# Edge walk of a graph attention layer: a register load moved, logit differences made by TensorE, sums kept in PSUM, a loop body four times as long

## The chip, the cores and the metric

The kernel runs on one core of a Trainium2 chip (trn2). The metric is the device time of one execution in microseconds (us); the kernel before has a median of 4355.9 us over three runs (4355.7 to 4357.51).

## What is computed

```python
# graph attention over 200000 edges sorted by dst, 6250 nodes, 8 heads of 32
q, k, v = (xn @ W + b).reshape(n, HEADS, D)            # three products
logits  = einsum('ehd,ehd->eh', q[dst], k[src]) / sqrt(D)
seg_max = segment_max(logits, dst)
expv    = exp(logits - seg_max[dst])
denom   = segment_sum(expv, dst)
agg     = segment_sum(expv / denom[dst] * v[src], dst)
out     = layernorm(x + gelu(agg + skip))
# then a second, smaller attention over 131072 edges routes each node to
# two of four expert networks, whose outputs are added with gates
```

Only the middle of the first half (logits, segment maxima and segment sums) is touched by the change.

## The kernel before, in words

The program has stages in sequence: `prepare` (projections of all nodes to DRAM, walk tables, and the sort of the second edge list), `attend` (the walk over the edges), `node_update`, `route_experts`, `route_gates`. The change lies in `attend` alone, and in the constant PASS (line 43).

**The walk.** Edges are sorted by destination and cut into 391 groups of 512 (G = 4 tiles of 128 edges). Destinations are cut into 49 blocks of 128 nodes. A turn handles one pair of group and node block; where a group spans two blocks it has two turns, so there are 391 + 49 - 1 = 439 turns, and a group has 439/391 = 1.12 turns in the mean. Tables in SBUF (`w_tab`, `g_tab`) give each turn its block and its group; each engine reads them into registers itself (`load`, line 725, a TENSOR_LOAD with an arithmetic operation and a range check behind it).

**What a turn does.** An edge's membership in the block is a one-hot matrix (`oh`, made by ScalarE, turned by TensorE into `ohT`). TensorE spreads the block's queries to edges (12 bf16 products, line 969, into PSUM tile Q). VectorE multiplies them with the gathered keys (`product`, 845) and sums over each head (`logits`, 849). TensorE turns the logits (978), VectorE runs a segmented maximum scan (799), TensorE turns it back (980), VectorE picks the segment ends (792), TensorE collects them per node (998 to 1003), VectorE reduces over the tiles (803) and raises the running maximum of the node block (`raise_max`, 816). TensorE spreads that maximum to the edges (`references`, 986); VectorE subtracts (`difference`, 807, one turn later); ScalarE takes the exponential (922) into the last column of each head of `msg`; VectorE multiplies the gathered values (`message`, 837). TensorE sums messages per node in f32 (1011, 8 instructions), adding the old sums that VectorE has scaled by the fall of the maximum (`scale_sums`, 832, product 1014 with the identity); ScalarE copies the result to the block's place in `acc` in SBUF (899).

**The order.** All of it is a software pipeline written out by hand: in the body for turn s, VectorE works on turns s-1 (message), s (maximum), s+1, s+2 (segment ends, scan) and s+4 (product, logits); TensorE has its own body with turns s-1 to s+7, ScalarE and SyncE likewise. Each engine's body is repeated by `walk` (707): two turns, a loop `Fori` whose body holds PASS = 36 turns, and 5 turns behind it. With 437 turns left after the first two, that is 12 passes. Inside a pass a register once loaded is kept for as many turns as it is needed; `enter` forgets all registers at the head of each pass. The last turn of a pass (`last`) loads nothing for the next.

**The gathers.** GpSimd is not in the loop; its program is unrolled. For each group it issues four indirect DMAs (742) that bring 512 rows of keys and values into a ring of KVR = 8 groups. A slot is free when `message` of its group's last turn is done (740). The group's arrival is passed on to VectorE by the semaphore `tiles` (733), after the four issues of the next group.

**PSUM.** Q takes four banks, `ohT_ps`, `turned_ps`, `node_ps` (references and maxima) and `agg_ps` one each.

Of the kernel before, what the change touches and what calls it, by code (L numbers as in the profile page):

```python
# [26 lines left out]
P = 128  # L27
# [15 lines left out]
PASS = 6 * LOOP  # L43
# [614 lines left out]
def attend(nc, k):  # L658
# [8 lines left out]
    with ExitStack() as ctx:  # L667
# [17 lines left out]
        dl = sb("dl", [P, TG], F32)  # L685
        msg = [sb(f"msg{i}", [P, G, HEADS, HW], F32) for i in range(2)]
        scaled = sb("scaled", [P, HEADS * HW], F32)
# [5 lines left out]
        node_ps = ps("node_ps", [P, 4, P], F32)  # L693
        ref_ps, max_ps = node_ps[:, 0, 0:TG], node_ps[:, 1, 0:TG]
        agg_ps = ps("agg_ps", [P, 512], F32)
        names = ("tiles", "used", "ring_seen", "off", "square", "oh", "turned", "ohT", "q", "prod", "lg", "running", "scans",
                 "seg_max", "maxima", "tile_max", "m_new", "m_fall", "m_all", "fac", "dl", "p", "msg", "oh32", "agg",
                 "scaled", "acc", "cleared", "resets_seen")
# [29 lines left out]
        with nc.Block() as block:  # L728
# [40 lines left out]
            def _(v):  # L769
# [35 lines left out]
                def difference(s):  # L805
                    v.wait_ge(ok["maxima"], s.v + 2)
                    v.tensor_tensor(dl[:, :], lg[s.slot][:, :], ref_ps, ALU.subtract).then_inc(ok["dl"], 1)  # L807

# [3 lines left out]
                def raise_max(s):  # L812
                    v.wait_ge(ok["tile_max"], s.v + 1)
                    if there(s + (-1)):
                        v.wait_ge(ok["m_all"], s.v)
                    v.tensor_tensor(m_new[:, :], node_max(s), tile_max[:, :], ALU.max).then_inc(ok["m_new"], 1)

                def fall(s):
                    v.wait_ge(ok["m_new"], s.v + 1)
                    v.tensor_tensor(m_fall[ring(s, 2)][:, :], node_max(s), m_new[:, :], ALU.subtract).then_inc(ok["m_fall"], 1)  # L820
# [5 lines left out]
                def sums(s):  # L826
                    return k.acc[:, bass.ds(window(s), 1), :].rearrange("p a (h e) -> p (a h) e", e=HW)
# [50 lines left out]
                v.memset(k.acc[:, :, :], 0.0).then_inc(ok["acc"], 1)  # L878
# [962 lines left out]
```

## Time and profile before

| | |
|---|---|
| runs | 4355.9 us median of 3 |
| profiled execution | span 4355.3 us |
| TensorE / VectorE busy in it | 79% / 80% |
| ScalarE / GpSimd busy in it | 58% / 61% |
| stage `prepare` | 0 to 338 us |
| the walk, first to last gather issue | 338.9 to 2667 us |
| the rest (node update, experts, gates) | to 4355 us |

The span holds five stages with different limits, so the shares of the whole say little of the walk; it has to be read in windows of its own. Of a timeline the first column is the start in us from the beginning of the span, the second how long the instruction (or the merged run of instructions) took; the bracket at the end, where there is one, says how long the engine stood idle before it and what ended that. "issue" means that the profile shows nothing that was waited for. Starts of successive VectorE instructions are closer together than the durations, since the next one starts before the last one has written everything; so costs are read from start to start.

### The profile page before, as it was taken

Reading aid. Unit: us, or ns where it says so; the run is one execution under the profiler, and the core shown is the slowest. Engines: PE = TensorE matmul, PEld = TensorE weight load, DVE = VectorE, ACT = ScalarE, POOL = GpSimd, SP = SyncE. Lnnn points to the kernel's source line nnn. Section 1 sums busy time; section 2 is a strip of 40 time slices with the busy share of each in tenths; the row PEclk is TensorE's granted clock in tenths of the full one; section 3 lists DMA queues with packets and bytes.
Section 4 is the critical chain, followed back from the end, with each engine's and each line's share of the span. In section 5 each row is a group of like instructions: output and inputs, shape, how many; then the busy total and the mean of one; then the engine's idle time right before and its main releaser. Section 6 shows DMA issues by size and latency. Waiting matters only on the chain. (4 is left out here: it accounts for less than half of the span.)

```text
span 4355.3 us, 107023 instructions
## 1 busy us (share of the span) xinstructions
PE 3439.8 (79%) x26106; PEld 2517.5 (58%) x26107; DVE 3480.0 (80%) x9712; ACT 2533.3 (58%) x6256; POOL 2677.3 (61%) x2719
## 2 busy tenths in 40 slices
PE   7887988889898988989898888248888888887620
PEld 3335777777777777777777676235555555555410
DVE  8887988889898988989898898866666666666457
ACT  5436766767676766767676676545555555555310
POOL 3226766666666666666666663227777777777740
PEclk9988999999999999999999999559999999999855
DMA  6537777767677767777776774611121111111147
GB/s 222 182 118 231 227 212 220 212 210 227 207 226 215 224 208 214 227 212 218 217 225 207 215 225 152 215 56 26 30 35 31 31 30 31 31 35 30 22 95 274
DMA packets 367763, 677.61 MB, mean 156 GB/s; under 512 B 70294, under 2 KB 240482, under 8 KB 367074
## 3 DMA queue, kind: packets, MB, share of 16 engines
q0 software_dynamic: 157888, 420.64, 35.2%
q1 hardware_dynamic: 183106, 223.48, 15.2%
q10 hardware_dynamic: 26080, 25.70, 2.0%
q8 instruction: 261, 4.28, 0.4%
q14 instruction: 428, 3.51, 0.3%
HBM read 582.00 MB, written 87.58 MB: 154 GB/s over the span
## 5 line engine op out<-in xcount | busy, mean ns | idle before, releaser
L742 POOL DMA_INDIRECT KV<-kv_d,src_i x1564 | 1558.6, 997 | 775.9 <-issue 437.0
L1385 POOL DMA_INDIRECT re_src<-src_tab_d,rsrc x1024 | 985.9, 963 | 312.1 <-issue 245.6
L1011 PE MATMUL agg_ps<-msg,oh 128*128 128x264 f32 x3512 | 865.2, 390 | 2.5 <-DVE msg L837 1.9
L837 DVE TENSOR_TENSOR msg<-KV,msg 128x1024 f32<-128x1024 f32 x439 | 537.9, 1225 | 225.1 <-issue 223.9
L1011 PEld LDWEIGHTS agg_ps<-msg,oh 128*128 128x128 f32 x3512 | 640.4, 192 | 98.8 <-ACT oh L926 2.0
L969 PE MATMUL Q<-q,ohT 128*128 128x256 bf16 x5328 | 672.4, 277 | 1.9 <-issue 0.9
L911 ACT ACTIVATE square<-iota_b,off 128x128 bf16<-128x128 bf16 x1784 | 569.4, 392 | 0.3
L845 DVE TENSOR_TENSOR prod<-KV,Q 128x1024 f32<-128x1024 f32 x443 | 537.8, 1214 | 5.1 <-POOLq L733 3.4
L849 DVE TENSOR_REDUCE lg<-prod 128x32 f32<-128x1024 f32 x443 | 535.0, 1208 | 0.2
L969 PEld LDWEIGHTS Q<-q,ohT 128*128 128x128 bf16 x5328 | 495.7, 99 | 64.2 <-issue 2.2
L922 ACT ACTIVATE msg<-dl 128x32 f32<-128x32 f32 x439 | 113.4, 258 | 662.3 <-DVE dl L807 662.3
L1593 PE MATMUL ex_y_ps<-ex_w,ex_hid 128*112 128x256 f32 x1792 | 441.2, 390 | 0.0
L1581 PE MATMUL ex_h<-acc,ex_w 128*128 (+1 forms) x896 | 413.9, 587 | 4.1 <-PEq L1094 3.5
L1512 ACT COPY re_ohT<-re_ohT_ps 128x1024 bf16<-128x1024 bf16 x179 | 181.2, 1012 | 348.8 <-PE re_ohT_ps L1555 348.0
L1593 PEld LDWEIGHTS ex_y_ps<-ex_w,ex_hid 128*112 128x112 f32 x1792 | 302.7, 179 | 53.8
L914 ACT ACTIVATE oh<-square,one 128x512 bf16<-128x512 bf16 x446 | 322.0, 722 | 14.5
L978 PE MATMUL turned_ps<-ident,lg 128*32 128x128 f32 x442 | 120.4, 272 | 257.2 <-DVE running L799 251.2
L926 ACT CAST oh<-oh 128x512 f32<-128x512 bf16 x439 | 272.0, 620 | 0.0
L1014 PE MATMUL agg_ps<-scaled,ident 128*128 128x264 f32 x878 | 267.1, 386 | 0.0
L1418 DVE TENSOR_SCALAR re_oh<-iota_b,re_off 128x128 bf16<-128x128 bf16 x1432 | 252.6, 274 | 6.4
L918 ACT COPY ohT<-ohT_ps 128x512 bf16<-128x512 bf16 x445 | 251.2, 564 | 4.8 <-PE ohT_ps L959 4.8
L1555 PE MATMUL re_ohT_ps<-ident_b,re_oh 128*128 128x128 bf16 x1432 | 120.4, 232 | 162.0 <-DVE re_oh L1418 157.7
(261 smaller groups left out, 5864.4 us busy)
## 6 DMA issues: line engine op xcount, KB each, us to landing
q<-q_d SPq DMA_DIRECT2D x446, 192.0 KB
y_d<-ex_y ACTq DMA_DIRECT2D x56, 448.0 KB
rg_ye<-y_d SPq DMA_DIRECT2D x7, 3584.0 KB, 12.5
KV<-kv_d,src_i POOLq DMA_INDIRECT x1564
nu_xs<-xs_d SPq DMA_DIRECT2D x7, 2688.0 KB, 11.7
re_src<-src_tab_d,rsrc POOLq DMA_INDIRECT x1024
kv_d<-pr_kv SPq DMA_DIRECT2D x49, 256.0 KB, 2.2
xs_d<-pr_xs SPq DMA_DIRECT2D x49, 256.0 KB, 2.3
```

Of the source, the lines that this page charges most:

```text
L742: pool.indirect_dma_start(out=KV[:, t % (KVR * G), :], out_offset=None, in_=k.kv_d, in_offset=bass.IndirectOffsetOnAxis(ap=k.src_i[:, t:t ...
L837: v.tensor_tensor(m[:, :, :, 0:DH], KV[:, tiles(s), D:2 * D].rearrange("p t (h d) -> p t h d", d=DH), bc(m[:, :, :, DH:HW], [P, G, HEADS, ...
L845: v.tensor_tensor(prod[:, :, :], KV[:, tiles(s), 0:D], Q[ring(s, 2)][:, :, :], ALU.mult).then_inc(ok["prod"], 1)
L849: v.reduce_sum(lg[s.slot][:, :], prod[:, :, :].rearrange("p t (h d) -> p (t h) d", d=DH), AX.X).then_inc(ok["lg"], 1)
L911: q = act.activation(square[:, t, :], k.iota_b[:, :], ACT.Square, bias=off[s.slot][:, t:t + 1])
L914: act.activation(oh[ring(s, OHR)][:, :, :], square[:, :, :], ACT.Relu, bias=k.one[:, :], scale=-1.0).then_inc(ok["oh"], 1)
L926: act.copy(oh32[ring(s, 2)][:, :, :], oh[ring(s, OHR)][:, :, :]).then_inc(ok["oh32"], 1)
L969: m = pe.matmul(Q[ring(s, 2)][:, t, :], ohT[ring(s, OHR)][:, t, :], q3[s.slot][:, c * D:(c + 1) * D], start=(c == 0), stop=(c == 2))
L1011: pe.matmul(agg_ps[:, 0:HEADS * HW], oh32[ring(s, 2)][:, t, :], msg[ring(s, 2)][:, t, :, :].rearrange("p h e -> p (h e)"), start=(t == 0), ...
L1385: pool.indirect_dma_start(out=gs[:, t % (RING * RG), :], out_offset=None, in_=k.src_tab_d, in_offset=bass.IndirectOffsetOnAxis(ap=k.rsrc[: ...
L1581: m = pe.matmul(h_ps[f % 2][:, 0:UN], k.w1_sb[:, u.at % NE, c, f * P:(f + 1) * P], k.xT[:, bass.ds(u.block, 1), c, half * UN:(half + 1) * ...
L1593: m = pe.matmul(y_ps[w % 2][0:YN, 0:D], hid[u.at % 2][:, f, w * YN:(w + 1) * YN], k.w2_sb[:, u.at % NE, f, :], start=(f == 0), stop=(f == ...
```

## The change

Four things are done at once:

1. VectorE's load of the next turn's block number (`window(s + 1)`) goes from behind `raise_max`, ahead of `message`, to behind `product`, ahead of `logits`.
2. VectorE's `difference` is gone. TensorE's `references` is now `differences`: it puts the logits into `dl_ps` through a product with the f32 identity (128x32) and adds the four spread maxima. For that the running maximum is kept with its sign turned (`raise_max` becomes one scalar_tensor_tensor, `fall` and the first value of `m_all` turn too). It waits until ScalarE has read the differences of the turn before. ScalarE's exponential reads `dl_ps` from PSUM.
3. The sums stay in `agg_ps`: `scale_sums` multiplies that tile in place and is placed right behind `message`; the two instructions of line 1014 are gone; `sums` waits for the scaling before its first product. ScalarE still copies the sums to `acc` in each turn, and `scale_sums` waits for the copy of the turn before. `acc` (49 x 264 columns) is no longer cleared; TensorE makes the first zeros in `agg_ps` by one product with 264 cleared columns. A new block's first fall is so large that its factor is 0.
4. PASS is 144 instead of 36: three passes instead of twelve, still 5 turns behind them.

`max_ps` moves into the bank of `turned_ps`; `dl_ps` has the bank that `node_ps` had.

```diff
-PASS = 6 * LOOP
+PASS = 24 * LOOP
...
-                def difference(s):
-                    v.wait_ge(ok["maxima"], s.v + 2)
-                    v.tensor_tensor(dl[:, :], lg[s.slot][:, :], ref_ps, ALU.subtract).then_inc(ok["dl"], 1)
...
-                    v.tensor_tensor(m_new[:, :], node_max(s), tile_max[:, :], ALU.max).then_inc(ok["m_new"], 1)
+                    v.scalar_tensor_tensor(out=m_new[:, :], in0=tile_max[:, :], scalar=-1.0, in1=node_max(s),
+                                           op0=ALU.mult, op1=ALU.min).then_inc(ok["m_new"], 1)
...
                 def scale_sums(s):
                     v.wait_ge(ok["fac"], s.v + 1)
-                    v.wait_ge(ok["acc"], s.v + 1)
-                    v.tensor_tensor(scaled[:, :].rearrange("p (h e) -> p h e", e=HW), sums(s), bc(fac[ring(s, 2)][:, :].unsqueeze(2), [P, HEADS, HW]), ALU.mult).then_inc(ok["scaled"], 1)
+                    if there(s + (-1)):
+                        v.wait_ge(ok["acc"], s.v)
+                    else:
+                        v.wait_ge(ok["emptied"], 1)
+                    sums = agg_ps[:, 0:HEADS * HW].rearrange("p (h e) -> p h e", e=HW)
+                    v.tensor_tensor(sums, sums, bc(fac[ring(s, 2)][:, :].unsqueeze(2), [P, HEADS, HW]), ALU.mult).then_inc(ok["scaled"], 1)
...
                 def body(s, last):
                     if there(s):
                         tile_maxima(s)
-                    if there(s + (-1)):
-                        difference(s + (-1))
                     if there(s + 1):
                         segment_max(s + 1)
                     if there(s + 2):
                         scan(s + 2)
                     if there(s):
                         raise_max(s)
-                    if there(s) and not last:
-                        window(s + 1)
                     if there(s + (-1)):
                         message(s + (-1))
+                        scale_sums(s + (-1))
                     if there(s):
                         fall(s)
                     product(s + 4)
-                    if there(s + (-1)):
-                        scale_sums(s + (-1))
+                    if there(s) and not last:
+                        window(s + 1)
                     logits(s + 4)
...
-                v.memset(k.acc[:, :, :], 0.0).then_inc(ok["acc"], 1)
-                v.memset(k.m_all[:, :, :], -BIG).then_inc(ok["cleared"], 1)
+                v.memset(msg[1][:, 0, :, :], 0.0).then_inc(ok["cleared"], 1)
+                v.memset(k.m_all[:, :, :], 2.0 * BIG).then_inc(ok["cleared"], 1)
...
-                def references(s):
+                def differences(s):
                     pe.wait_ge(ok["m_new"], s.v + 1)
+                    if there(s + (-1)):
+                        pe.wait_ge(ok["p"], s.v)
+                    pe.matmul(dl_ps, k.ident[:, :], lg[s.slot][:, :], start=True, stop=False)
                     for t in range(G):
-                        pe.matmul(ref_ps[:, t * HEADS:(t + 1) * HEADS], ohT[ring(s, OHR)][:, t, :], m_new[:, :], start=True, stop=True)
+                        m = pe.matmul(dl_ps[:, t * HEADS:(t + 1) * HEADS], ohT[ring(s, OHR)][:, t, :], m_new[:, :],
+                                      start=False, stop=(t == G - 1))
+                    m.then_inc(ok["dl"], 1)
...
-                    pe.wait_ge(ok["acc"], s.v + 1)
+                    pe.wait_ge(ok["scaled"], s.v + 1)
                     for t in range(G):
-                        pe.matmul(agg_ps[:, 0:HEADS * HW], oh32[ring(s, 2)][:, t, :],
-                                      msg[ring(s, 2)][:, t, :, :].rearrange("p h e -> p (h e)"), start=(t == 0), stop=False)
-                    pe.wait_ge(ok["scaled"], s.v + 1)
-                    pe.matmul(agg_ps[:, 0:HEADS * HW], k.ident[:, :], scaled[:, :], start=False, stop=True).then_inc(ok["agg"], 1)
+                        m = pe.matmul(agg_ps[:, 0:HEADS * HW], oh32[ring(s, 2)][:, t, :],
+                                      msg[ring(s, 2)][:, t, :, :].rearrange("p h e -> p (h e)"), start=False, stop=(t == G - 1), skip_group_check=True)
+                    m.then_inc(ok["agg"], 1)
```

## Rows read from the trace of the kernel before

**Rows 1.** Windows view, one pass: busy us (instructions) PE, PEld, DVE, ACT, POOL; clock, DMA, GB/s.
```profile
555.40:747.60 192.20, 170.30 (x1478) 137.98 (x1476) 169.21 (x397) 133.14 (x396) 127.32 (x128) 0.98 0.72 217
```
**Rows 2.** Timeline of VectorE, one ordinary turn and the head of the next.
```profile
2005.84 0.18 DVE L803 TENSOR_REDUCE tile_max<-node_ps 128x8 f32<-128x32 f32 x1
2005.94 0.18 DVE L807 TENSOR_TENSOR dl<-lg,node_ps 128x32 f32<-128x32 f32 x1
...
2006.13 0.40 DVE L799 TENSOR_TENSOR_SCAN running<-reset,turned_ps 32x128 f32<-32x128 f32 x1
2006.46 0.13 DVE L816 TENSOR_TENSOR m_new<-m_all,tile_max 128x8 bf16<-128x8 f32 x1
2007.03 1.23 DVE L837 TENSOR_TENSOR msg<-KV,msg 128x1024 f32<-128x1024 f32 x1 [0.44 <-issue]
2008.17 0.16 DVE L820 TENSOR_TENSOR m_fall<-m_all,m_new 128x8 f32<-128x8 bf16 x1
2008.25 1.22 DVE L845 TENSOR_TENSOR prod<-KV,Q 128x1024 f32<-128x1024 f32 x1
2009.38 0.43 DVE L832 TENSOR_TENSOR scaled<-acc,fac 128x264 f32<-128x264 f32 x1
2009.72 1.21 DVE L849 TENSOR_REDUCE lg<-prod 128x32 f32<-128x1024 f32 x1
2010.92 0.31 DVE L803 TENSOR_REDUCE tile_max<-node_ps 128x8 f32<-128x32 f32 x1
```
**Rows 3.** Timeline of VectorE, the last turn of the last pass (loads nothing).
```profile
2675.48 0.18 DVE L803 TENSOR_REDUCE tile_max<-node_ps 128x8 f32<-128x32 f32 x1
...
2676.10 0.13 DVE L816 TENSOR_TENSOR m_new<-m_all,tile_max 128x8 bf16<-128x8 f32 x1
2676.20 1.23 DVE L837 TENSOR_TENSOR msg<-KV,msg 128x1024 f32<-128x1024 f32 x1
...
2680.09 0.18 DVE L803 TENSOR_REDUCE tile_max<-node_ps 128x8 f32<-128x32 f32 x1
```
**Rows 4.** Timeline of VectorE: the jump between two passes, and the next pass's end.
```profile
752.76 0.31 DVE L803 TENSOR_REDUCE tile_max<-node_ps 128x8 f32<-128x32 f32 x1
...
760.81 0.19 DVE L803 TENSOR_REDUCE tile_max<-node_ps 128x8 f32<-128x32 f32 x1 [3.23 <-issue]
...
790.36 0.18 DVE L803 TENSOR_REDUCE tile_max<-node_ps 128x8 f32<-128x32 f32 x1
...
944.87 0.31 DVE L803 TENSOR_REDUCE tile_max<-node_ps 128x8 f32<-128x32 f32 x1
```
**Rows 5.** Timeline of TensorE, the same ordinary turn.
```profile
2006.68 0.27 PE L978 MATMUL turned_ps<-ident,lg 128*32 128x128 f32 x1 [0.43 <-DVE running L799]
...
2008.74 1.95 PE L1011 MATMUL agg_ps<-msg,oh 128*128 128x264 f32 x8
2010.52 0.61 PE L1014 MATMUL agg_ps<-scaled,ident 128*128 128x264 f32 x2
2010.97 0.39 PE L959 MATMUL ohT_ps<-ident_b,oh 128*128 128x128 bf16 x4
2011.76 0.27 PE L978 MATMUL turned_ps<-ident,lg 128*32 128x128 f32 x1 [0.41 <-DVE running L799]
```
**Rows 6.** Timeline of ScalarE, the same ordinary turn.
```profile
2006.29 0.36 ACT L899 COPY acc<-agg_ps 128x264 f32 x1
```
**Rows 7.** Timeline of GpSimd, first issues of two successive groups in the start.
```profile
349.28 0.94 POOL L742 DMA_INDIRECT KV<-kv_d,src_i  x1 [0.30 <-issue]
...
354.29 0.95 POOL L742 DMA_INDIRECT KV<-kv_d,src_i  x1 [0.30 <-issue]
```
**Rows 8.** Waits of GpSimd, 560 to 2640 us: us in total, times, longest us.
```profile
POOL KV L742 <- DVE msg L837: 276.5, 65, 6.7
```
**Rows 9.** Timeline of VectorE, the start of the walk.
```profile
340.87 10.84 DVE L878 MEMSET acc<- 128x12936 f32 x1 [3.05 <-issue]
...
364.19 1.22 DVE L845 TENSOR_TENSOR prod<-KV,Q 128x1024 f32<-128x1024 f32 x1 [2.10 <-POOLq L733]
```

More of the change, by code:

```diff
@@ L684, in attend @@
         fac = [sb(f"fac{i}", [P, HEADS], F32) for i in range(2)]
-        dl = sb("dl", [P, TG], F32)
         msg = [sb(f"msg{i}", [P, G, HEADS, HW], F32) for i in range(2)]
-        scaled = sb("scaled", [P, HEADS * HW], F32)
         KV = sb("KV", [P, KVR * G, 2 * D], F32)
@@ L692, in attend @@
         lgT_ps, runT_ps = turned_ps[0:TG, 0, :], turned_ps[:, 1, 0:TG]
-        node_ps = ps("node_ps", [P, 4, P], F32)
-        ref_ps, max_ps = node_ps[:, 0, 0:TG], node_ps[:, 1, 0:TG]
+        max_ps = turned_ps[:, 2, 0:TG]
+        dl_ps = ps("dl_ps", [P, 512], F32)[:, 0:TG]
         agg_ps = ps("agg_ps", [P, 512], F32)
-        names = ("tiles", "used", "ring_seen", "off", "square", "oh", "turned", "ohT", "q", "prod", "lg", "running", "scans",
+        names = ("tiles", "used", "off", "square", "oh", "turned", "ohT", "q", "prod", "lg", "running", "scans",
                  "seg_max", "maxima", "tile_max", "m_new", "m_fall", "m_all", "fac", "dl", "p", "msg", "oh32", "agg",
-                 "scaled", "acc", "cleared", "resets_seen")
+                 "scaled", "acc", "cleared", "emptied", "resets_seen")
         ok = {n: nc.alloc_semaphore(f"at_{n}") for n in names}
@@ L815, in raise_max @@
                         v.wait_ge(ok["m_all"], s.v)
-                    v.tensor_tensor(m_new[:, :], node_max(s), tile_max[:, :], ALU.max).then_inc(ok["m_new"], 1)
+                    v.scalar_tensor_tensor(out=m_new[:, :], in0=tile_max[:, :], scalar=-1.0, in1=node_max(s),
+                                           op0=ALU.mult, op1=ALU.min).then_inc(ok["m_new"], 1)
                 def fall(s):
                     v.wait_ge(ok["m_new"], s.v + 1)
-                    v.tensor_tensor(m_fall[ring(s, 2)][:, :], node_max(s), m_new[:, :], ALU.subtract).then_inc(ok["m_fall"], 1)
+                    v.tensor_tensor(m_fall[ring(s, 2)][:, :], m_new[:, :], node_max(s), ALU.subtract).then_inc(ok["m_fall"], 1)
                 def keep_max(s):
@@ L824, in keep_max @@
                     v.tensor_scalar(node_max(s), m_new[:, :], 1.0, None, ALU.mult).then_inc(ok["m_all"], 1)
-                def sums(s):
-                    return k.acc[:, bass.ds(window(s), 1), :].rearrange("p a (h e) -> p (a h) e", e=HW)
                 def scale_sums(s):
                     v.wait_ge(ok["fac"], s.v + 1)
-                    v.wait_ge(ok["acc"], s.v + 1)
-                    v.tensor_tensor(scaled[:, :].rearrange("p (h e) -> p h e", e=HW), sums(s), bc(fac[ring(s, 2)][:, :].unsqueeze(2), [P, HEADS, HW]), ALU.mult).then_inc(ok["scaled"], 1)
+                    if there(s + (-1)):
[4 more added lines that the diff above has]
+                    v.tensor_tensor(sums, sums, bc(fac[ring(s, 2)][:, :].unsqueeze(2), [P, HEADS, HW]), ALU.mult).then_inc(ok["scaled"], 1)
                 def message(s):
@@ L876, in body @@
                         group(s + 5)
-                v.memset(k.acc[:, :, :], 0.0).then_inc(ok["acc"], 1)
-                v.memset(k.m_all[:, :, :], -BIG).then_inc(ok["cleared"], 1)
-                v.wait_ge(ok["cleared"], 1)
+                v.memset(msg[1][:, 0, :, :], 0.0).then_inc(ok["cleared"], 1)
+                v.memset(k.m_all[:, :, :], 2.0 * BIG).then_inc(ok["cleared"], 1)
+                v.wait_ge(ok["cleared"], 2)
                 walk(v, body, 4, enter)
                 enter()
-                difference(LAST)
                 message(LAST)
@@ L921, in weights @@
                     act.wait_ge(ok["dl"], s.v + 1)
-                    act.activation(msg[ring(s, 2)][:, :, :, DH:HW], dl[:, :].rearrange("p (t h a) -> p t h a", h=HEADS, a=1), ACT.Exp,
+                    act.activation(msg[ring(s, 2)][:, :, :, DH:HW], dl_ps.rearrange("p (t h a) -> p t h a", h=HEADS, a=1), ACT.Exp,
                                    scale=SCALE).then_inc(ok["p"], 1)
@@ L1019, in body @@
                     if there(s):
-                        references(s)
+                        differences(s)
                     if there(s + 1):
@@ L1029, in body @@
                         group(s + 2)
+                pe.wait_ge(ok["cleared"], 1)
+                pe.matmul(agg_ps[:, 0:HEADS * HW], k.ident[:, :], msg[1][:, 0, :, :].rearrange("p h e -> p (h e)"),
+                          start=True, stop=True).then_inc(ok["emptied"], 1)
                 walk(pe, body, 7, groups.clear)
```

## Prediction, on record before the changed kernel ran

> **What bounds the kernel now.** I read the page first, then windows by stage, then timelines of one turn on each engine. The page's shares of 79% TensorE and 80% VectorE do not tell which of the two sets the pace, since they are averages over five stages. The window of one pass of 36 turns does better: 192.2 us, a TensorE clock of 0.98 of full speed (so its upper level, 2.4 GHz, nearly throughout), DMA engines 72% busy [rows 1]. From the head of a turn to the head of the next VectorE works without a hole except one: 5.08 us from L803 to L803, in which only `message` (L837) has idle time before it, 0.44 us [rows 2]. TensorE waits once in the turn, for VectorE's scan, 0.41 to 0.43 us [rows 5]. So VectorE sets the pace of the walk; TensorE follows with little to spare. The reader should see that the hole of 0.44 us is called "issue": no semaphore is late, the engine's own sequencer is still busy with the register load that stands ahead of `message` in the program.
>
> The mean ordinary turn is a little over 5.08: thirty turns from 790.36 to 944.87 take 154.51 us, 5.15 each [rows 4].
>
> **Part 1, the load behind `product`.** The kernel before has turns in which this load is missing: the last turn of a pass loads nothing. There L837 starts 0.10 us after L816 instead of 0.57, and the turn takes 4.61 us from L803 to L803 instead of 5.08 [rows 2, 3]. That is the gain to expect, 0.47 us a turn, if the load is hidden in its new place. Its cover there is `product`, 1.13 us from start to start (2008.25 to 2009.38) [rows 2]; the load cost 0.47 of visible time where nothing but the end of a short instruction covered it, so it fits into 1.13 even if it is somewhat longer than what was visible. The instruction behind it, `logits`, has to wait for the end of `product` anyway. If the cover failed (the sequencer reaching the load only when `product` ends) the 0.47 would come back ahead of `logits`.
>
> **Part 2, differences by TensorE.** `difference` occupied VectorE from 2005.94 for about 0.10 us until its successor (L792 starts at the same pitch as L807 behind L803, 0.10) [rows 2]. It goes: 0.10 us a turn. The sign turns cost nothing: one instruction for one, on the same 8 columns.
>
> TensorE gets one f32 product of 32 columns through the identity, as two instructions. No row shows such a one. Bounds: the two instructions of L1014, with the same 128x128 f32 weights but 264 columns, take 0.45 together (2010.52 to 2010.97); at the other end if only the columns counted, 32 of 264 would make it 0.45/8, that is 0.05 [rows 5]. I take 0.25, nearer to the wide weights than to the few columns. The Trainium skill ("TensorE: Matmul & The Clock Gate", section "LDWEIGHTS (loading the stationary operand)") makes a load of 128 columns 128/1.2 = 107 ns, so an estimate by that page is 0.21 us for the two; the sum does not use it.
>
> ScalarE now gets its differences a turn's length earlier than it can use them, from PSUM as it already reads `agg_ps`. At nothing.
>
> **Part 3, sums in PSUM.** TensorE loses the two instructions of L1014, 0.45 us a turn [rows 5]. VectorE's scaling has the same 264 columns; it reads and writes PSUM now. For reading there is a pair of rows: `product` has one operand in PSUM and its successor starts 1.13 us later, `message` has all in SBUF and its successor starts 1.14 us later [rows 2]. So reading costs nothing. No row has VectorE write to PSUM; as upper bound I take the whole pitch of a tiny instruction again, 0.08 us (L820 to L845) [rows 2], lower bound 0; I take 0, since the operand rows show no difference. The Trainium skill says otherwise for operands ("VectorE: DVE Perf Modes", section "The TRN2 errata — SBUF-src ops pay a fixed extra latency per instruction"): a fixed part of 120 cycles from PSUM against 58 from SBUF at 0.96 GHz. That would be 0.065 us a turn, an estimate of 28 us over the walk by this page, and the sum would come out at 4080. The pair of rows above shows nothing of such a difference, so I go by the rows.
>
> The scaling moves ahead of TensorE's eight products, so there is a new chain from turn to turn: scaling, eight products (1.78 from first start to the next instruction, and their latency) [rows 5], ScalarE's copy 0.36 [rows 6], scaling again 0.43 [rows 2]. That is about 3 us, under a turn. In phase it also holds: `message` ends 0.1 us before L820's successor; the products of the turn before have ended by the time TensorE comes to its wait for the scan, the copy follows in half a microsecond, and the scaling comes only 1.2 us after the scan. What queues behind the scaling on VectorE, should it wait, is everything: `fall`, `product`, `logits`.
>
> TensorE's turn: its path without the wait is 5.08 less 0.41 less what the overlap of the last product allows (about 0.15), 4.5 us. Less 0.45, plus 0.25: 4.3, at the upper bound 4.5. VectorE's turn will be 5.15 - 0.47 - 0.10 = 4.58. So VectorE stays the bound, with 0.1 to 0.3 us to spare.
>
> The clearing of `acc` (10.84 us) goes at the start of the walk [rows 9]. It is worth nothing or little: the fourth product, at 364.19, waits 2.10 us for gathers, which GpSimd issues at its own speed from 338.9 on. I count 0; if gathers were not late, at most 10.8.
>
> **Part 4, three passes for twelve.** The jump back costs: six turns from 752.76 to 790.36 take 37.60 us where six ordinary ones of 5.12 (the commonest length in the timeline) take 30.72, so 6.9 us [rows 4]; of that 3.23 is a standstill at the jump, the rest is spread over the next five turns, in which registers are loaded anew and instructions arrive late. The window of the pass says the same: 192.2 us less 36 x 5.15 leaves 6.8 [rows 1]. There are eleven such jumps; counted in this manner over the timeline they cost 6.7 to 7.7, mean 7.04. Two will be left. Nine fewer: 9 x 7.04 = 63.3 us. The entry into the loop and the way out of it stay. I take the cost of a jump as independent of the body's length, since the standstill follows the jump and not the instructions before it.
>
> **The sum.** 438 intervals x 0.57 = 249.7; jumps 63.3; together 313. From this I take off 9 for the gathers, as follows. GpSimd issues a group in 5.01 us (349.28 to 354.29) [rows 7]. With 391 groups to 439 turns that is 4.46 us a turn against 4.58: not the bound, but near. Before, GpSimd stood 276.5 us of 2080 waiting for `message` [rows 8]; that reserve shrinks to some 2%. In a stretch of eight turns without a shared group VectorE wants eight groups in 36.6 us and GpSimd needs 40.1, so it falls behind by 3.5, and catches up in the ninth turn. The ring gives three turns of lead, 13.7 us, from the end of `message` of one group to `product` of the group eight later. In the start, where VectorE waits for them, a group's gathers take 9.9 us from their first issue to its product (354.29 to 364.19) [rows 7, 9]. That leaves 3.8 against the 3.5 by which it falls behind: enough, with now and then a hitch. Nine microseconds, 0.2 for each of 49 node blocks, is my estimate for the hitches and for the start.
>
> The profiled execution has a span of 4355.3 us, and the median of the runs is 4355.9, so both differ by 0.6 and the saving can be taken from the median: 4355.9 - 313 + 9 = 4052 us.
>
> **Rivals.**
>
> *Gathers set the pace* (15%). For it: the reserve of 2% above, and DMA engines that are already 72% busy [rows 1] and have to move the same bytes in 0.89 of the time, near 80%, so that landings may come later. Against: the mean is still under VectorE's. Its time: a turn of 4.68 instead of 4.58, 44 us more, so about 4096, and 4110 if landings take 2 us longer.
>
> *TensorE or the PSUM write set the pace* (14%). For it: both bounds above together, TensorE at 4.5 and each handover late by 0.1 to 0.2; or 0.08 more for the write. Its time: 0.08 to 0.12 a turn, 35 to 53 us, so 4087 to 4105. Against: TensorE loses more than it gets.
>
> *The change doesn't do what it says: the load shows again in front of `logits`* (4%). Then 0.47 x 438 = 206 us come back: 4258. Against: the turns without load, and 1.13 us of cover.
>
> *Slower than before* (3%): the chain through `agg_ps`. VectorE's whole stream stands behind the scaling, the scaling behind ScalarE's copy, the copy behind TensorE's last product of the turn before. If ScalarE came to the copy late, behind its one-hot work, each turn would grow. The point from which it decides: the jumps saved are worth 63.3/438 = 0.14 a turn, so from a turn of 5.15 + 0.14 = 5.29 on the kernel is slower. At a turn of 5.4 it would take 4355.9 + 0.11 x 438 = 4404. Against: the chain adds up to 3 us, and ScalarE's order (weights, copy, then the rest) keeps the copy early.
>
> *Better than forecast* (6%): the small irregularities over 5.08 go too, 0.05 a turn, 4030 or a little less.
>
> **How the numbers follow.** The forecast, 4040 to 4070, has 58%. The range takes in the gathers' and TensorE's cases and the lucky one: 4028 to 4112, leaving out about 4% below and 13% above. A difference under 0.2% (8.7 us) could not be told from none by this measurement; none of the cases but the chain's edge lies there. Faster 0.96, same 0.01, slower 0.03.
>
> **What would show it.** In the changed profile: `message` 0.1 to 0.2 us behind `raise_max`, without idle time before it (part 1); no VectorE instruction between L803 and the segment ends, and the new f32 product within 0.05 to 0.45 on TensorE (part 2); the scaling at a pitch of 0.34 as before (part 3); three standstills of 3 to 4 us on VectorE at most instead of eleven, each with its 7 us (part 4); GpSimd's wait for `message` shrunk from 276 to under 100 us, VectorE rarely waiting for `KV`. Wrong would be: idle time before `product` that ends with gathers in most turns, idle time before the scaling that ends with ScalarE's copy, or idle time before `logits`.

## The result, and the profile after

The changed kernel takes 4241.1 us (median of four runs, 4232.8 to 4248.9), against 4356.7 us of the kernel before in the same comparison: a ratio of 0.9731, interval 0.9716 to 0.9746. In a second comparison on a chip of the same speed it took 4232.7 us, 0.9714 (0.9698 to 0.9731). It is faster by 116 to 123 us, where 304 were forecast; 4241 lies above the whole range. All times below are of executions in the chip's faster state; one, of the changed kernel with passes of 36 turns, took 5439.7 us at a granted TensorE clock of 0.55 against 0.91 to 0.92 in its like, and is left out.

All of it is in the walk. Between the first `tile_max` of the walk and the last (367.19 and 2580.33) lie 2213.1 us, 122.6 less than before (2335.7), or 5.05 us for each of 438 intervals where 4.64 were forecast (jumps and the 9 us for gathers included). The stages behind the walk, which the change doesn't touch, took 1653.0 us before and 1654.6 after (1653.3 in a second profile of the changed kernel); over the versions told below on chips of this speed they vary from 1641 to 1655. So differences of some ten us between versions are read from the walk, not from the whole time.

VectorE's timeline of an ordinary turn of the changed kernel (columns as in [rows 2]):

```profile
1500.24 0.18 DVE L801 TENSOR_REDUCE tile_max<-turned_ps 128x8 f32<-128x32 f32 x1
1500.34 0.18 DVE L790 SCALAR_TENSOR_TENSOR seg_max<-last_b,turned_ps 128x32 bf16<-128x32 f32 x1
1500.44 0.40 DVE L797 TENSOR_TENSOR_SCAN running<-reset,turned_ps 32x128 f32<-32x128 f32 x1
1500.77 0.13 DVE L810 SCALAR_TENSOR_TENSOR m_new<-tile_max,m_all 128x8 bf16<-128x8 f32 x1
1500.82 1.21 DVE L833 TENSOR_TENSOR msg<-KV,msg 128x1024 f32<-128x1024 f32 x1
1501.96 0.42 DVE L828 TENSOR_TENSOR agg_ps<-agg_ps,fac 128x264 f32<-128x264 f32 x1
1502.30 0.14 DVE L815 TENSOR_TENSOR m_fall<-m_new,m_all 128x8 f32<-128x8 bf16 x1
1502.38 1.20 DVE L841 TENSOR_TENSOR prod<-KV,Q 128x1024 f32<-128x1024 f32 x1
1503.61 1.22 DVE L845 TENSOR_REDUCE lg<-prod 128x32 f32<-128x1024 f32 x1
...
1504.82 0.18 DVE L801 TENSOR_REDUCE tile_max<-turned_ps 128x8 f32<-128x32 f32 x1
...
1505.40 1.20 DVE L833 TENSOR_TENSOR msg<-KV,msg 128x1024 f32<-128x1024 f32 x1
...
1517.45 1.22 DVE L841 TENSOR_TENSOR prod<-KV,Q 128x1024 f32<-128x1024 f32 x1 [0.86 <-POOLq L731]
```

This turn takes 4.58 us from L801 to L801, to the hundredth what was forecast (in part by luck, see below). `message` starts 0.05 behind `raise_max` with no idle time (0.57 in [rows 2]). But in the fourth turn from here `product` has stood 0.86 us for L731, the semaphore that says that the group's rows are there. Of the 438 turns 207 are such ordinary ones of 4.58 or 4.59 us; the others are longer, up to 7 us outside the jumps, most often with a wait for rows in them.

The waits of the changed kernel from 560 to 2500 us (us in total, times, longest us), those of VectorE:

```profile
DVE prod L841 <- POOLq L731: 82.4, 95, 2.4
DVE prod L841 <- PE Q L961: 32.5, 29, 2.1
...
DVE agg_ps L828 <- ACT acc L891: 19.1, 26, 2.3
...
DVE tile_max L801 <- issue: 6.8, 2, 3.5
```

GpSimd's wait for `message`, 276.5 us in [rows 8], does not occur in this stretch at all. So the roles have changed: before, GpSimd waited for VectorE; now it never does, and VectorE waits for it.

GpSimd's timeline in the same stretch shows why it doesn't keep up:

```profile
1499.83 0.95 POOL L740 DMA_INDIRECT KV<-kv_d,src_i  x1 [0.30 <-DMA KV<-kv_d,src_i]
1501.08 1.77 POOL L740 DMA_INDIRECT KV<-kv_d,src_i  x1 [0.30 <-issue]
1503.16 0.95 POOL L740 DMA_INDIRECT KV<-kv_d,src_i  x1 [0.31 <-issue]
1504.41 0.95 POOL L740 DMA_INDIRECT KV<-kv_d,src_i  x1 [0.30 <-issue]
1505.67 1.77 POOL L740 DMA_INDIRECT KV<-kv_d,src_i  x1 [0.30 <-issue]
1507.74 0.95 POOL L740 DMA_INDIRECT KV<-kv_d,src_i  x1 [0.31 <-issue]
1508.99 0.94 POOL L740 DMA_INDIRECT KV<-kv_d,src_i  x1 [0.30 <-issue]
1510.24 1.77 POOL L740 DMA_INDIRECT KV<-kv_d,src_i  x1 [0.30 <-issue]
```

Every third issue takes 1.77 us instead of 0.95. It is the one that starts 0.26 us after `message` (1501.08 against 1500.82, 1505.67 against 1505.40). Three issues, one of them long, fill exactly one turn: 1505.67 - 1501.08 = 4.59. So the pattern keeps itself in step as long as VectorE runs undisturbed, and GpSimd then needs 4/3 of 4.58, 6.11 us, for a group. VectorE uses up the lead and waits for rows (1511.92, for 0.32 us, and 1517.45, for 0.86); by that the phase slips, and issues run free for a while.

The kernel before has the same long issue, seldom. Its GpSimd timeline at such a place:

```profile
1949.13 0.95 POOL L742 DMA_INDIRECT KV<-kv_d,src_i  x1 [0.30 <-issue]
1950.38 1.98 POOL L742 DMA_INDIRECT KV<-kv_d,src_i  x1 [0.31 <-issue]
```

and its VectorE timeline at the same place:

```profile
1950.32 1.23 DVE L837 TENSOR_TENSOR msg<-KV,msg 128x1024 f32<-128x1024 f32 x1 [0.45 <-issue]
```

Over all issues behind the first `message`, sorted by how long after the start of the last `message` each begins (worked out from the two timelines; mean duration in us, number in brackets):

| start after `message`, us | before | changed | message reads weights from PSUM |
|---|---|---|---|
| 0.0 to 0.2 | 1.92 (11) | 1.79 (26) | 0.945 (60) |
| 0.2 to 0.4 | 1.69 (13) | 1.76 (242) | 0.945 (54) |
| 0.4 to 0.6 | 1.55 (27) | 1.52 (42) | 0.945 (80) |
| 0.6 to 0.8 | 1.39 (14) | 1.32 (19) | 0.945 (39) |
| 0.8 to 1.0 | 1.07 (231) | 1.13 (35) | 0.946 (50) |
| later | 0.95 to 1.02, and seven of 1.10 to 1.22 | 0.95 to 0.96 | 0.945 |

The last column is an experiment, told below. In the first two, start and duration add up to the same: an issue that begins 0.06 to 1.08 us after `message` began ends 2.03 us after that start (2.05 in the kernel before, whose `message` is 0.02 longer), and so 0.82 after `message` itself (1.21 long) has ended. An issue that begins outside this stretch isn't lengthened, not even just ahead of it: 46 issues of the changed kernel that begin in the last 0.13 us before a `message` take 0.942 to 0.952, and three that begin 0.01 after its start take 0.942 to 0.947 (they are in the first row's mean). That fits an issue that comes, about 0.13 us after its own start (0.95 less 0.82), to something that `message` holds until its end. What that is no row shows. From when on it is held differs: ahead of the second half of a `message` in two parts (an experiment below) issues that begin up to 0.06 us before it are long too. `message` itself does not get longer: 1.207 us in the mean beside an issue of over 1.2 us, 1.214 without one.

The seven late ones in the kernel before obey the same law with another instruction. They begin 0.03 to 0.15 us after `scale_sums`, which there reads both its operands, `acc` and `fac`, from SBUF, and each ends 0.82 us after it has ended. GpSimd's and VectorE's line of one of them:

```profile
1947.66 1.16 POOL L742 DMA_INDIRECT KV<-kv_d,src_i  x1 [0.39 <-issue]
```
```profile
1947.58 0.42 DVE L832 TENSOR_TENSOR scaled<-acc,fac 128x264 f32<-128x264 f32 x1
```

In the changed kernel, whose `scale_sums` reads the sums from PSUM, no issue that begins over 1.1 us after `message` takes more than 0.97.

The groups of instructions (line, count, busy us and mean ns | idle before, by what), GpSimd's gathers in the changed kernel:

```profile
L740 POOL DMA_INDIRECT KV<-kv_d,src_i x1564 | 1738.2, 1111 | 483.4 <-issue 444.4 <-DMA KV<-kv_d,src_i 34.1 <-POOLq L197 4.8
```

and in the kernel before:

```profile
L742 POOL DMA_INDIRECT KV<-kv_d,src_i x1564 | 1558.6, 997 | 775.9 <-issue 437.0 <-DVE msg L837 291.7 <-DMA KV<-kv_d,src_i 42.4
```

1738.2 + 483.4 us are 2221.6, and that is the walk: the gathers are issued without any wait for VectorE from first to last. A turn's share is 2221.6/439 = 5.06, measured 5.05. Undisturbed it would be 1564 x (0.946 + 0.309) = 1963 us, 4.47 a turn, under VectorE's 4.58: that was the forecast's picture.

### The profile page after: what moved, and what is told of

It reads as the page before. It is cut to its first block and busy times, and to the rows that moved or that the text cites. A ratio compares the mean times of both kernels' runs of the same rounds, so it can differ in the third digit from the quotient of the medians.

```text
span 4234.9 us, 106026 instructions
## 1 busy us (share of the span) xinstructions
PE 3355.8 (79%) x26108; PEld 2461.8 (58%) x26109; DVE 3429.0 (81%) x9273; ACT 2556.3 (60%) x6256; POOL 2860.5 (68%) x2719
## 3 DMA queue, kind: packets, MB, share of 16 engines
q1 hardware_dynamic: 183106, 223.48, 15.4%
## 5 line engine op out<-in xcount | busy, mean ns | idle before, releaser
L740 POOL DMA_INDIRECT KV<-kv_d,src_i x1564 | 1738.2, 1111 | 483.4 <-issue 444.4
L1008 PE MATMUL agg_ps<-msg,oh 128*128 128x264 f32 x3512 | 882.1, 395 | 1.6 <-DVE agg_ps L828 1.6
L1008 PEld LDWEIGHTS agg_ps<-msg,oh 128*128 128x128 f32 x3512 | 656.1, 197 | 102.2 <-ACT oh L918 1.7
L961 PE MATMUL Q<-q,ohT 128*128 128x256 bf16 x5328 | 691.4, 282 | 0.5 <-issue 0.3
L891 ACT COPY acc<-agg_ps 128x264 f32 x439 | 166.5, 379 | 474.4 <-PE agg_ps L1008 473.3
L1417 DVE TENSOR_SCALAR re_oh<-iota_b,re_off 128x128 bf16<-128x128 bf16 x1432 | 258.2, 278 | 11.5 <-issue 4.3
L1554 PEld LDWEIGHTS re_ohT_ps<-ident_b,re_oh 128*128 128x128 bf16 x1432 | 87.9, 103 | 247.4 <-DVE re_oh L1417 213.7
```

The lines of the kernel that those rows point to most:

```text
L740: pool.indirect_dma_start(out=KV[:, t % (KVR * G), :], out_offset=None, in_=k.kv_d, in_offset=bass.IndirectOffsetOnAxis(ap=k.src_i[:, t:t ...
L961: m = pe.matmul(Q[ring(s, 2)][:, t, :], ohT[ring(s, OHR)][:, t, :], q3[s.slot][:, c * D:(c + 1) * D], start=(c == 0), stop=(c == 2))
L1008: m = pe.matmul(agg_ps[:, 0:HEADS * HW], oh32[ring(s, 2)][:, t, :], msg[ring(s, 2)][:, t, :, :].rearrange("p h e -> p (h e)"), start=False ...
```

## The experiments

Theory A: `message` with two operands in SBUF stands in the way of the gathers' issues, by the phase law above, and the issues set the pace. Its rivals: B, the DMA engines, which now move 229 GB/s instead of 217 [rows 1], make landings late; C, it is PSUM or TensorE's side of the new chain.

Seven of the runs (told below as "on the slower chips") were made on two chips on which every kernel takes over 5800 us (the kernel before 5954 on the one, 5917 on the other), so that VectorE is late and GpSimd waits for it by far the longest; their times don't bear on the question, and only the durations of their issues are used.

### Message reads its weights from PSUM

ScalarE takes the exponential a second time, into the spare half of the bank of `ohT_ps`, and `message` multiplies with that. It adds waits: TensorE's turn of a one-hot waits for the exponential, `message` for that turn, ScalarE's `turn_copy` for `message`.

```diff
+        w_ps = ohT_bank[:, G, 0:2 * TG].bitcast(F32)
...
                 def message(s):
                     v.wait_ge(ok["p"], s.v + 1)
+                    v.wait_ge(ok["turned"], s.v + 8)
...
-                                    bc(m[:, :, :, DH:HW], [P, G, HEADS, DH]), ALU.mult).then_inc(ok["msg"], 1)
+                                    bc(w_ps.rearrange("p (t h a) -> p t h a", h=HEADS, a=1), [P, G, HEADS, DH]), ALU.mult).then_inc(ok["msg"], 1)
...
                 def weights(s):
+                    act.activation(w_ps, dl_ps, ACT.Exp, scale=SCALE)
```

> The changed kernel, but message reads the edge weights from PSUM (ScalarE writes them there by a second exponential), so it has one operand in SBUF instead of two. Theory A (a gather's issue on GpSimd stands still while message runs, because message reads two operands from SBUF; in the changed kernel 3 gathers instead of 4 get through per turn of 4.58 us): the gathers of 1.77 us disappear, mean issue 0.95 to 0.98 us instead of 1.11, mean turn 4.58 to 4.68 instead of 5.05, time 4050 to 4095 us. Rival B (the DMA queues: 420 MB of rows can't land faster): issue times and time stay as in the changed kernel, 4225 to 4245. Rival C (GpSimd's own pace of four issues is the bound, blocked or not): little gain, 4200 to 4240.

On a slower chip: 5856.5 us against 5954.3, ratio 0.983 (0.978 to 0.988). The mean issue is 946 ns; of 1564 only the first of all is long, as in every kernel (1.30).

> As e1, weights of message from PSUM. Theory A: 4050 to 4095 us where the kernel before takes 4356, gathers 0.95 us each, mean turn 4.58 to 4.68 us. Rivals B (DMA volume) and C (four issues of 1.25 us are too slow anyway): no faster than the changed kernel by more than 40 us.

Measured: 4103.8 us, ratio 0.9418 (0.9402 to 0.9434); 129 to 137 us less than the changed kernel, 9 above what A expected. Its group of gathers:

```profile
L742 POOL DMA_INDIRECT KV<-kv_d,src_i x1564 | 1478.9, 946 | 609.4 <-issue 445.5 <-DVE msg L836 128.0 <-DMA KV<-kv_d,src_i 31.1
```

and its window of 560 to 2400 us (columns as in [rows 1]):

```profile
560.00:2400.00 1840.00, 1717.37 (x15861) 1404.93 (x15859) 1786.87 (x3866) 1479.93 (x4641) 1299.60 (x1375) 1.00 0.80 243
```

GpSimd again waits for `message`, 128 us, and the DMA engines are busier than in the changed kernel, whose window of 560 to 2500 us is:

```profile
560.00:2500.00 1940.00, 1751.83 (x15773) 1428.06 (x15772) 1771.18 (x3847) 1442.49 (x4229) 1521.19 (x1368) 0.97 0.77 229
```

243 GB/s against 229, and VectorE never waits for rows in that window: B is out. A turn is still longer than 4.58 (most take 4.58 to 4.75, the mean with jumps is 4.77). That fits the waits that the edit adds: `message` starts 0.12 to 0.15 us behind `raise_max` around 1505 us, where the changed kernel has 0.05.

### Message in two halves

`message` is two instructions of 512 columns, `scale_sums` between them. Each half holds issues for half as long.

```diff
+                    for a in (0, 2):
+                        w = v.tensor_tensor(m[:, a:a + 2, :, 0:DH], KV[...][:, a:a + 2], bc(m[:, a:a + 2, :, DH:HW], [P, 2, HEADS, DH]), ALU.mult)
+                        if a == 0:
+                            scale_sums(s)
+                    w.then_inc(ok["msg"], 1)
...
                         message(s + (-1))
-                        scale_sums(s + (-1))
```

> The changed kernel, message in two instructions of 512 columns with the scaling of the sums (one operand in PSUM) between them. Theory A: the longest standstill of a gather is halved, longest usual issue 1.3 to 1.5 us instead of 1.77, mean 1.00 to 1.05, mean turn 4.7 to 4.85, time 4090 to 4150. Rival B: no gain, and 0.06 us a turn more on VectorE that is hidden: 4225 to 4245.

On a slower chip: 5832.9 us (two runs), ratio 0.978 (0.972 to 0.984), mean issue 990 ns, a little under the 1.00 to 1.05 expected.

> As e3, message in two halves with the scaling between. Theory A: usual delayed issue 1.24 us (as in e3) instead of 1.77, mean gather 1.00 to 1.03, 4070 to 4150 us where the kernel before takes 4356. Rival B: as the changed kernel.

Measured: 4098.1 us, ratio 0.9408 (0.9392 to 0.9424), faster than both kernels. Its walk is as long as that with weights from PSUM (2087.8 and 2088.3 us from the first `tile_max` to the last); the 6 us between the two are behind the walk. The group of gathers:

```profile
L740 POOL DMA_INDIRECT KV<-kv_d,src_i x1564 | 1592.1, 1018 | 501.6 <-issue 438.9 <-DMA KV<-kv_d,src_i 32.0 <-DVE msg L834 25.8
```

And VectorE's timeline, around one of the few waits for rows:

```profile
1501.58 0.67 DVE L834 TENSOR_TENSOR msg<-KV,msg 128x512 f32<-128x512 f32 x1
1502.18 0.42 DVE L828 TENSOR_TENSOR agg_ps<-agg_ps,fac 128x264 f32<-128x264 f32 x1
1502.52 0.67 DVE L834 TENSOR_TENSOR msg<-KV,msg 128x512 f32<-128x512 f32 x1
1503.12 0.15 DVE L815 TENSOR_TENSOR m_fall<-m_new,m_all 128x8 f32<-128x8 bf16 x1
1503.87 1.22 DVE L845 TENSOR_TENSOR prod<-KV,Q 128x1024 f32<-128x1024 f32 x1 [0.60 <-POOLq L731]
```

The half costs 0.60 from start to start, so a turn has 0.06 more of VectorE. The issues and their gaps, the 25.8 us of waiting for `message` left out, come to (1.018 + 0.304) x 4 = 5.29 a group, 4.71 a turn; the mean turn is 4.77 (2087.8/438). Even here the issues and VectorE (4.64 to 4.70 in most turns) are nearly level.

### Half the bytes

Each gather brings the keys only, 1 KB for each row instead of 2; `message` multiplies the keys. The values are left out; number and length of all instructions stay.

```diff
-                        pool.indirect_dma_start(out=KV[:, t % (KVR * G), :], out_offset=None, in_=k.kv_d,
+                        pool.indirect_dma_start(out=KV[:, t % (KVR * G), 0:D], out_offset=None, in_=k.kv_d,
```

> The changed kernel with gathers of 1 KB rows instead of 2 KB (message multiplies the keys' half again instead of the values): as many issues, half the bytes. Theory A: the same time as the changed kernel within 20 us and the same 1.11 us a gather. Rival B: 100 us or more faster.

Measured: 4245.9 us (two runs), ratio 0.9746 (0.9727 to 0.9766), like the changed kernel, and the issues as long, though the DMA engines now move 136 GB/s instead of 229 in the window of 560 to 2500 us:

```profile
L740 POOL DMA_INDIRECT KV<-kv_d,src_i x1564 | 1752.7, 1121 | 482.0 <-issue 466.5 <-DMA KV<-kv_d,src_i 10.7 <-POOLq L197 4.8
```

What a gather brings plays no part. B is refuted from the other side too.

### The changed kernel again

> The changed kernel itself, so that the runs beside it have their like on the same chip. On a chip like that of the first measurement 4225 to 4250 us against 4356 before, all gathers issued without waiting for message, 1.11 us a gather. On a chip like that of the runs e1 to e4 (before 5954 us) some 5850 to 5900.

4232.7 us, mean issue 1111 ns: the result stands.

### The changed kernel with passes of 36 turns

```diff
-PASS = 24 * LOOP
+PASS = 6 * LOOP
```

> As e9, for a chip on which the kernel before takes 4356 us: the changed kernel with PASS = 36. Theory A: 0 to 25 us over the changed kernel's 4233 to 4241, so 4235 to 4265. Rival (each jump 7 us in any case): about 4298.

Measured: 4243.2 us, ratio 0.974 (0.972 to 0.976), 2 to 11 us more. The walk itself takes 2232.7 us against 2213.1 and 2215.0 in the two profiles of the changed kernel: nine more jumps cost 18 to 20 us there, 2.0 to 2.2 each, and not 63. They are still there on VectorE (turns of 8.2, 7.0, 5.9 and 5.4 us at one), but GpSimd's program is unrolled and goes on issuing meanwhile, and VectorE waits less for rows, as this kernel's waits from 560 to 2500 us show (82.4 us in the changed kernel):

```profile
DVE prod L841 <- POOLq L731: 68.1, 68, 2.7
```

### Weights from PSUM, passes of 36 turns

> As e10: weights of message from PSUM and PASS = 36. VectorE bounds this walk, so the nine jumps cost 50 to 65 us over 4104: 4154 to 4169.

Measured: 4211.0 us, ratio 0.9668 (0.9652 to 0.9684), 107 us more, of which 103.9 are in the walk (2192.2 us against 2088.3): where gathers are not in the way, nine jumps cost 11.5 us each, 104 together where 50 to 65 were expected. Most of the excess is the edit's added wait, which is long at a jump:

```profile
562.93 1.22 DVE L836 TENSOR_TENSOR msg<-KV,ohT_ps 128x1024 f32<-128x1024 f32 x1 [3.90 <-PE ohT_ps L959]
```

The waits of `message` for TensorE, from 400 to 2560 us, grow by it from 15.4 us with two jumps to 59.0 with eleven, 4.8 for each. Without them a jump costs 6.7, near the prediction's 7.04. The expectation's size was wrong; that the jumps are dear here and cheap in the changed kernel held.

### Single parts in the kernel before

Only the pass of 144 turns:

> As e11: the kernel before with PASS = 144 alone. Theory A: 45 to 63 us gained, 4293 to 4311. If gathers were the bound already: under 20 us.

Measured: 4282.0 us, ratio 0.9826 (0.981 to 0.9843): 75 us less, 11 below the lower end of what was expected. The walk is shorter by 64.9 us (2270.9 against 2335.7), 7.2 for each of nine jumps, and part 4 said 63.3 and 7.04; the rest lies behind the walk, where this kernel took 1641.7 us and the kernel before 1653.0. GpSimd's wait for `message` stays the long one, from 560 to 2500 us (261.2 in the same window of the kernel before):

```profile
POOL KV L742 <- DVE msg L837: 194.9, 45, 5.4
```

Only the load moved:

```diff
-                    if there(s) and not last:
-                        window(s + 1)
                     if there(s + (-1)):
                         message(s + (-1))
                     if there(s):
                         fall(s)
                     product(s + 4)
+                    if there(s) and not last:
+                        window(s + 1)
```

> As e12: the kernel before with the load behind product alone. If VectorE's own turn (4.61 to 4.68 us) counted, 4150. Theory A: three issues into such a turn, 4235 to 4290, issues of 1.77 us, mean 1.09 to 1.12.

Measured: 4284.6 us, ratio 0.983 (0.9813 to 0.9846), within what theory A expected: 73 us less, where 438 x 0.47 = 206 of VectorE's time are removed. Without any other part of the change the issues already grow, to a mean of 1145 ns, more than the 1.09 to 1.12 us expected:

```profile
L742 POOL DMA_INDIRECT KV<-kv_d,src_i x1564 | 1790.6, 1145 | 488.0 <-issue 456.1 <-DMA KV<-kv_d,src_i 26.5 <-POOLq L197 4.8
```

and GpSimd's wait for `message` is gone, VectorE's for rows is there (waits from 560 to 2500 us):

```profile
POOL KV L742 <- DVE msg L837: 0.6, 2, 0.3
...
DVE prod L845 <- POOLq L733: 73.1, 88, 2.8
```

This excludes C: neither the differences nor the sums in PSUM are in this kernel, and it falls short in the same way.

### The same kernels on a slower chip

The changed kernel with passes of 36 turns, once on each of the two:

> The changed kernel with PASS = 36 again (eleven jumps instead of two). Theory A: the gathers go on while VectorE stands at a jump, so the jumps cost little in a walk that the gathers bound: 0 to 25 us more, 4235 to 4265. Rival (each jump costs its 7 us in any case, as the prediction had it): 63 us more, about 4298.

> The changed kernel with PASS = 36 (nine jumps more). Theory A (gathers bound the walk, blocked by message): GpSimd goes on issuing while VectorE stands at a jump, so the jumps cost little: 0 to 25 us over the changed kernel's 4233 to 4241, so 4235 to 4265. Rival (each jump costs 7 us in any case): about 4298.

Measured: 6002.2 us, ratio 1.0074 (1.0051 to 1.0097), and 5975.0 us, 1.0103 (1.0065 to 1.0141). Weights from PSUM with the short pass:

> Weights of message from PSUM, with PASS = 36. Here VectorE's turn bounds the walk, not the gathers, so the nine jumps should cost what they cost before: 50 to 65 us over 4104, so 4154 to 4169. If they cost under 25 us, the price of a jump in the prediction was wrong for itself.

Measured: 5890.6 us, 0.9965 (0.9932 to 0.9998). The kernel before with the long pass:

> The kernel before with PASS = 144 alone. Theory A: GpSimd had 276 us of waiting in reserve and is in step with the turn, so most of the nine jumps is gained: 45 to 63 us, 4293 to 4311. If gathers were the bound already: under 20 us.

Measured: 5921.3 us, 1.0003 (0.9976 to 1.0029). The load alone:

> The kernel before with the load behind product alone. VectorE's turn by itself 4.61 to 4.68 us, which would be 206 us less if nothing else bound it (4150). Theory A: the gathers get three issues into such a turn, so it ends where the changed kernel ends: 4235 to 4290, issues of 1.77 us, mean 1.09 to 1.12, product waiting for gathers.

Measured: 6000.0 us, 1.0145 (1.01 to 1.019). The expectations of a time were made for a chip on which the kernel before takes 4356 us, and all are missed here. The gathers of the changed kernel with passes of 36 turns (the first of the two):

```profile
L740 POOL DMA_INDIRECT KV<-kv_d,src_i x1564 | 1513.8, 968 | 1732.3 <-DVE msg L833 1291.5 <-issue 432.4 <-POOLq L197 4.8
```

GpSimd waits 1291.5 us for `message`: the gathers are not the limit there, so these runs say nothing of the term in question. What differs is TensorE: its granted clock from 560 to 2500 us is 0.81 to 0.85 in the seven runs, where the changed kernel has 0.97. Two of its turns in the same kernel show the same eight instructions, the first at a granted clock of 0.50 (the lower level, 1.2 GHz), the second at 1.00:

```profile
1499.53 3.86 PE L1008 MATMUL agg_ps<-msg,oh 128*128 128x264 f32 x8
...
1506.08 1.95 PE L1008 MATMUL agg_ps<-msg,oh 128*128 128x264 f32 x8
```

## Why the prediction was wrong

**The step that failed** is in the sum: "GpSimd issues a group in 5.01 us (349.28 to 354.29) [rows 7] ... 4.46 us a turn against 4.58: not the bound, but near". The rows are from the start of the walk, where `message` does not run yet; there nothing disturbs an issue. In the walk an issue of 0.95 us costs up to 1.98 when it begins just behind the start of `message`. In the changed kernel the mean is 1.111, a group costs (1.111 + 0.309) x 4 = 5.68 us, a turn 5.06. With that number in the sum the walk is 2222 us instead of 2032, and the time 4355.9 - (2335.7 - 2222) = 4242 us; measured 4241. This one term is enough for the miss, since the gathers, issued without any wait for VectorE, are as long as the walk. That the rest of the sum would have given 4052 isn't shown: the two versions whose issues are freed take 4098 and 4104, each with costs of its own on VectorE.

What let it pass: the kernel before has only some 65 long issues (mean 997 ns). Its GpSimd waited for the end of `message` now and then [rows 8], and four issues with their gaps then come to 3 x 0.95 + 1.07 + 4 x 0.30 = 5.12, the commonest turn of that kernel. That fits a pattern in which one issue in four meets the last part of `message` (231 issues at 0.8 to 1.0 us behind its start), at a cost of 0.1, and which a faster turn breaks; the pattern is inferred from these sums, and no run tests it by itself. The forecast saw that the reserve would shrink to 2%, and priced its loss by landings and bytes (4096 to 4110). The rival "gathers set the pace" had the right engine and the wrong cause, with a price of 4.68 where 5.05 came.

The Trainium skill ("SBUF — State Buffer", section "Who interferes with whom") has the rule: a VectorE instruction with two SBUF inputs contends with a GpSimd instruction that reads SBUF. The prediction did not weigh it: `message` has two SBUF inputs, the issue takes its indices from `src_i`, a tile in SBUF. This case's traces agree: 0.945 us in every phase when one input comes from PSUM, up to 1.98 when both are in SBUF. That it is a port that the issue lacks is an inference; the runs show only that the place of the operand decides.

**The other steps, one by one.**
- Part 1, the load: the mechanism is right. `message` starts 0.05 behind `raise_max`, without idle time. But what parts 1 and 3 do together to `logits` was put at nothing: it waits for the end of `product`, and `scale_sums`, which stood between the two, has moved away. So `product` now takes 1.23 us to the next start instead of 1.13 (1502.38 to 1503.61). The turn of [rows 2] loses 0.52 ahead of `message` and 0.09 for `difference`, and gets 0.10 back here: from 5.08 to 4.58 are 0.50, where the sum has 0.57, 31 us over the walk. That 4.58 was met all the same is luck: the sum took its 0.57 from the mean of 5.15, the trace shows 0.50 off the undisturbed 5.08.
- Part 2: right, 0.09 to 0.10 less on VectorE. TensorE's f32 product takes 0.24 from start to start (taken 0.25):

```profile
1501.36 0.41 PE L979 MATMUL dl_ps<-lg,ident 128*128 128x32 f32 x2
1501.60 0.24 PE L981 MATMUL dl_ps<-m_new,ohT 128*128 128x8 bf16 x4
```

- Part 3: right. The scaling in PSUM has a pitch of 0.34 (1501.96 to 1502.30), as in SBUF [rows 2]; the 0.065 that the prediction worked out from the Trainium skill ("VectorE: DVE Perf Modes", section "The TRN2 errata — SBUF-src ops pay a fixed extra latency per instruction") did not appear. One reading there is off without effect: `message` ends at 2008.26, 0.01 after L820's successor starts and not 0.1 before it [rows 2]. The clearing of `acc` was worth nothing: the first `tile_max` lies at 367.19, and lay at 366.58 before.
- Part 4: the jump's cost on VectorE is as read, two standstills of up to 3.5 us are left between 560 and 2500 us (L801, `issue`). Its worth depends on who sets the pace, read from the walk: 7.2 us a jump in the kernel before (7.04 forecast), 11.5 with weights from PSUM, 4.8 of it in the added wait, and 2.0 to 2.2 in the changed kernel. The prediction took it as independent of the body's length; what it depends on here is the neighbour engine.
- The gains don't add up: the pass alone shortens the walk by 64.9 us and the load alone by 66.4 (2269.4), together 131, and the whole change, parts 2 and 3 included, by 122.6. Once the load is hidden the gathers are the limit, with the rest of the change or without it.
- Rivals: TensorE or the PSUM write, load shown again, chain through `agg_ps`: none set the pace. The waits of `scale_sums` for ScalarE's copy are 19.1 us in 26 cases from 560 to 2500 us, those of `product` for TensorE 32.5 in 29; every one of them lies in a walk that the gathers fill anyway.

**Left open**: why the issues' mean is 1111 and not, say, 1050; it was taken from the trace, not derived from the phase law. What it is that `message` and an issue share. Why the unchanged stages behind the walk vary by 14 us between versions. And why TensorE's clock is lower on the slower chips, and the load alone made the kernel slower there.

## What to carry to other kernels

An engine that keeps up by 2% has been priced in the state in which it waits; before shortening its neighbour, sort the durations of its instructions by their phase against the neighbour's, and bound its cost from the worst phase as well (here 4/3 of 4.58, 6.11 us a group, against 5.01). A saving on one engine is only worth what the next limit leaves, so two measured savings may be worth less together than the sum. When a long elementwise instruction with two SBUF operands runs beside indirect gathers, cut it in two or put one operand into PSUM: here that gave another 129 to 143 us. And when a part of the program that wasn't touched varies by as much as an effect, read the effect from the part that was: a jump looked 8.4 us dear by the whole time (75/9) and is 7.2 by the walk.

## What the hardware showed that was not expected

- An indirect gather's issue on GpSimd takes 0.95 us for 128 rows and 0.30 to the next, whether the rows have 2 KB or 1 KB (1111 and 1121 ns in the mean under the same disturbance); begun 0.06 to 1.08 us after a 1.21 us `tensor_tensor` with both operands in SBUF, it ends 0.82 us after that one's end; behind a 0.43 us one of that kind (`scale_sums` in the kernel before) as well. With one operand in PSUM nothing is lengthened (0.945 us in every phase), and the `tensor_tensor` isn't slowed.
- GpSimd and VectorE lock in phase: 211 of the issues in the changed kernel take 1.74 to 1.80 us, nearly all of them 0.25 to 0.27 us behind the start of `message`.
- One jump of the loop costs 7.2 us of the walk where the gathers don't hide it, 2.0 to 2.2 where they do, and 11.5 in the kernel in which `message` also waits for TensorE, 4.8 of it in that wait.
- `logits` stands 0.10 us longer behind `product` when nothing is placed between them: 1.23 us from start to start against 1.13 to the instruction that stood there before.
